# A decoder layer: the last group's output product by channel blocks over seven banks, tile 0 normed first, and the first scores by quarters

## The chip, the cores and the metric

The kernel runs on 1 core of one Trainium2 chip. The metric is the device time of one execution in microseconds. The engines are TensorE (PE, matmuls; PEld its weight loads), VectorE (DVE), ScalarE (ACT), GpSimd (POOL) and the queue of SyncE (SP), which issues most transfers.

## The reference

One post-norm decoder layer on 16 sequences of 56 tokens (896 rows of 512 values, all float32), with three parts, each followed by a layer norm of x + part:

```python
# 1. a state-space mixer: 128 heads of 64, 8 groups
h = x * rsqrt(mean(x*x) + 1e-5) * norm_w
gate, hBC, dt = split(h @ in_proj_w.T)            # 8192, 8192 + 2*1024, 128
hid, B, C = split(silu(causal_conv4(hBC) + conv_b))
dt = softplus(dt + dt_bias);  A = -exp(A_log)
y = ((C @ B.T) * exp(segsum(A * dt))) @ (hid * dt) + Dp * hid   # per head, causal
yg = y * silu(gate)
yg = yg * rsqrt(mean over each of the 8 groups of 1024 channels (yg*yg) + 1e-5) * gnorm_w
x = layernorm(x + (x + yg @ out_proj_w.T))
# 2. attention of the 56 tokens over a context of 1500 rows, context both key and value
x = layernorm(x + softmax(x @ ctx.T) @ ctx)
# 3. x @ W_base.T + b_base plus the two best of 8 low-rank experts (rank 16)
x = layernorm(x + base + lora)
```

## The kernel before, in words

**Mixer.** The 896 tokens are 7 tiles of 128 (TT = 7). The 8192 inner channels are 8 groups of 8 blocks of 128 (GROUPS, CT). For each group g and step st, PE projects one block of hid and one of gate (L1132), and for the block before it transposes hid (`transpose_hid`, L1143), DVE scales it (`scale_hid`) and weighs the decay matrix (`weigh`), and PE makes the block's y (`y_product`, L1156). DVE adds the skip term (`add_skip`, L794), then multiplies by the gate (`multiply_gate`, L807). To multiply in full precision with fast matmuls, y and the output weights are split in a high and a low part: ACT makes y_hi (L582) and wo_hi (L600), DVE wo_lo (L814), POOL y_lo (L414). ACT squares y (L593) and POOL adds the squares (L421).

**Output product.** It is y times w_out, three matmuls (high-high, high-low, low-high) for each token tile and channel block. For each group it goes in two halves of four blocks. `first_half` (step 5) goes tile by tile over two PSUM banks, `ob`, and ACT copies each tile to `part`. `second_half(g)` does the blocks 4 to 7 of group g - 1 in step 1 of group g: all four blocks of a tile, then the next tile, in the two banks in turn, so that a tile waits for DVE to have read the one two before it. Before it, PE sums the squares over the channels with a matrix of ones (`sum_squares`, L1192), from which DVE (`group_squares`) and POOL (`group_rms`, L426) make the group's scale rg. For each tile DVE adds the two halves (L875) and adds rg times them to `acc` (L878). The last group has its second half in a pseudo-group 8 of two steps (`group(GROUPS, 2)`), in which no projection runs.

**Norm 1 and attention.** In that pseudo-group, after each tile's sum, DVE makes the layer norm's statistics (`norm1_stats`, L899 to L904), POOL the scale and shift (L476, L478) and ACT the normed tile (`first_norm`, L673). The attention goes over 8 pairs of sequences. A pair's tokens are copied from `acc` to `x1p` by DMAs that POOL issues (`load_x1`, L460), padded to 64 rows a sequence. PE transposes them (`turn_queries`, L1203), and ACT spreads them over qT with 16 copies of 32 rows (`queries`, L687), quarter by quarter (c of 0 to 3). The context comes in units of 2 MB (three a pair, a ring of six: ring_a, ring_b) from SP (`load_unit`, L340). DVE transposes each unit in 32 by 32 blocks to keysT (`keys_part(u, r, half)`, two instructions, L886). PE makes the scores with 128 products of 32 rows by 64 columns, each over 384 keys and run as two instructions, in four row strips (`score`, L1285). DVE takes the maximum (`score_max`, L966), ACT the exponential (L703), PE transposes it (`turn_probs`, L1324) and multiplies by the context (`values`, L1336), DVE adds x1p (`norm2_sum`, L980). The feed-forward part of a pair runs under the scores and values of the next.

The order of the work is written out by hand for each engine; semaphores join the engines. In a pair, PE does score(u), turn_x2(u-1), turn_queries(u+1), feed_forward(u-1), turn_probs(u, 0 to 2), values(u, 0 to 2). DVE does the norms of pair u-1, keys_part(u+1, 0, 0), score_max(u), keys_part(u+1, 0, 1), the first probabilities' copy, the routing, four more key parts, and norm2_sum(u). POOL does rstd2(u-1), load_x1(u+1), rstd3 and the store of pair u-2. PSUM has eight banks: 0 to 3 take projections and later scores and transposed probabilities, 4 and 5 take y and later `turn` and `pv`, 6 and 7 are `ob` and later `ffn` and `misc`.

## Time and profile before

| | |
|---|---|
| median of 3 runs (lowest, highest) | 1488.67 us (1488.58, 1489.81) |
| the profiled execution, its time | 1492.33 us |
| the profiled execution, its span | 1490.6 us |
| mean granted TensorE clock | 0.981 |
| last projection's matmul starts | 1169.09 us |
| six context transfers (6 MB) are issued from | 1170.07 us |

The page gives for each engine its busy time, its share of the span and the number of instructions. A granted clock of 1.00 is 2.4 GHz, 0.50 is 1.2 GHz. Timelines give start (us from the span's start), duration, engine, line, operation, written and read tiles, and in brackets the idle time before with what ended it. Some matmul records can be missing.

**Single operations** in that trace (us):

| operation | duration |
|---|---|
| add_skip L794, two instructions | 1.27 |
| weigh L847; multiply_gate L807 | 1.08; 1.09 |
| scale_hid L825, two instructions | 1.29 |
| wo_lo L814: median, longest of 64 | 0.75, 2.58 |
| y_hi L582; sq L593 (ACT) | 0.95; 0.94 |
| y_lo L414; squares' sum L421 (POOL) | 2.08; 2.09 |
| transposes of hid L1143, eight | 1.07 |
| sum of squares at full clock L1192, eight | 0.59 |
| group_squares L860, L863, L865 | 0.39, 0.39, 0.17 |
| half sum L875; sum L878 | 0.69; 0.75 |
| statistics L899, L901, L903, L904 | 0.69, 0.18, 0.15, 0.15 |
| POOL's rstd L476; shift L478 | 0.56; 0.19 |
| first_norm L673 | 0.81 |
| transposes L1203, four | 0.66 |
| maximum L966; exponential L703 with its accumulator read | 1.76; 1.54 + 0.19 |
| x1p load's issue L460, three on POOL | 1.73 |

### The profile page before, as it was taken

The numbers are of one execution on the slowest core, as the hardware profiler recorded it, in microseconds if no ns is written. First come the engines' busy times: TensorE is split into PE (matmuls) and PEld (weight loads), VectorE is DVE, ScalarE is ACT, GpSimd is POOL, SyncE is SP. The second block draws the span as 40 slices with busy tenths as digits, with TensorE's granted clock in tenths as the row PEclk, the third lists the DMA queues.
The fourth block names the chain that finished last, engine by engine and source line by source line (L and its number), as shares of the span: only waits on it lengthen the run. The fifth ranks groups of instructions, "written<-read, shape, count | busy, mean of one in ns | idle before, by whom it ended". The sixth has DMA issues, their size and how long they took to land.

```text
span 1490.6 us, 29598 instructions
## 1 busy us (share of the span) xinstructions
PE 1424.6 (96%) x12540; PEld 1164.9 (78%) x12540; DVE 996.9 (67%) x1312; ACT 751.9 (50%) x1003; POOL 501.6 (34%) x368
## 2 busy tenths in 40 slices
PE   5899999999999999999999999999999779999895
PEld 4798989898889888888988898989898554445452
DVE  5774768476847675676577566747683776888764
ACT  5764636563746364636554564455455344533340
POOL 5252435242534243433343343425243320112001
PEclk9999999999999999999999999999999889999997
DMA  4431213121312131222122221222130455566600
GB/s 149 121 104 53 80 56 99 54 89 42 97 58 86 46 102 54 73 58 89 55 72 65 83 72 54 84 64 86 40 97 23 184 202 207 207 255 259 178 19 13
DMA packets 53345, 142.57 MB, mean 96 GB/s; under 512 B 9777, under 2 KB 9905, under 8 KB 46951
## 3 DMA queue, kind: packets, MB, share of 16 engines
q1 hardware_dynamic: 51518, 137.01, 27.9%
q0 software_dynamic: 1696, 3.67, 0.8%
q8 instruction: 99, 1.62, 0.5%
q14 instruction: 32, 0.26, 0.1%
HBM read 136.53 MB, written 2.29 MB: 93 GB/s over the span
## 4 chain that ended last, share of the span: by engine, by line
PE 85%; issue 7%; DVE 4%; DMA 2%; ACT 1%; POOL 1%; POOLq 0%; ACTq 0%; DVEq 0%
PE bank L1113 46%; PE bank L1181 21%; PE bank L1156 5%; PE bank L1143 4%; PE bank L1336 3%; PE bank L1285 2%; PE bank L1309 2%; DMA x1p<-acc 1%; DVE conv L780 1%; PE bank L1305 1%; PE bank L1168 1%; PE bank L1324 0%; DVE part L741 0%; DMA part<-in_x 0%; PE bank L1192 0%
## 5 line engine op out<-in xcount | busy, mean ns | idle before, releaser
L1113 PE MATMUL bank<-h_hi,w_hi 128*128 128x448 f32 x1152 | 338.1, 375 | 2.2 <-DVE conv L780 2.2
L414 POOL TENSOR_TENSOR y_lo<-yg,y_hi 128x896 fp32r<-128x896 f32 x64 | 136.2, 2127 | 581.5 <-ACT y_hi L582 541.4
L1113 PE MATMUL bank<-h_lo,w_hi 128*128 128x448 f32 x1152 | 328.0, 366 | 0.0
L1113 PE MATMUL bank<-h_hi,w_lo 128*128 128x448 f32 x1152 | 327.2, 365 | 0.0
L780 DVE SCALAR_TENSOR_TENSOR conv<-bank,conv_w,conv 128x880 f32<-128x880 f32 (+2 forms) x240 | 267.9, 1117 | 85.2 <-ACT conv L555 79.4
L1113 PEld LDWEIGHTS bank<-h_hi,w_lo 128*128 128x128 f32 x1152 | 216.8, 188 | 17.4
L1113 PEld LDWEIGHTS bank<-h_lo,w_hi 128*128 128x128 f32 x1152 | 216.9, 188 | 17.1
L398 POOL TENSOR_TENSOR w_lo<-w_raw,w_hi 128x512 fp32r<-128x512 f32 x144 | 188.3, 1308 | 119.0 <-ACT w_hi L521 117.5
L1113 PEld LDWEIGHTS bank<-h_hi,w_hi 128*128 128x128 f32 x1152 | 208.2, 188 | 20.0 <-DVE conv L780 2.6
L825 DVE TENSOR_TENSOR hd_dt<-bank,dt_j 128x512 f32<-128x512 f32 x128 | 82.3, 685 | 209.0 <-PE bank L1143 209.0
L1181 PE MATMUL bank<-wo_hi,y_hi 128*128 128x512 f32 x448 | 178.6, 399 | 7.9 <-POOL y_lo L414 3.8
L1181 PE MATMUL bank<-wo_lo,y_hi 128*128 128x512 f32 x448 | 176.5, 394 | 0.0
L1181 PE MATMUL bank<-wo_hi,y_lo 128*128 128x512 f32 x448 | 176.0, 393 | 0.0
L582 ACT ACTIVATE y_hi<-yg 128x896 fp32r<-128x896 f32 x64 | 60.9, 951 | 205.0 <-DVE yg L807 204.7
L562 ACT ACTIVATE hid<-conv 128x896 f32<-128x896 f32 x64 | 61.0, 953 | 150.4 <-DVE conv L780 150.2
L421 POOL TENSOR_TENSOR sqsum<-sq,sqsum 128x896 f32<-128x896 f32 x56 | 119.8, 2140 | 0.0
L1181 PEld LDWEIGHTS bank<-wo_hi,y_hi 128*128 128x128 f32 x448 | 85.1, 190 | 29.9 <-issue 6.2
L555 ACT ACTIVATE conv<-bank,conv_b,conv_w 128x896 f32<-128x896 f32 x80 | 87.0, 1088 | 31.7 <-PE bank L1113 31.6
L1285 PE MATMUL bank<-keysT,qT 32*64 32x384 f32 (+1 forms) x2048 | 88.0, 485 | 13.2 <-DVE keysT L886 9.6
L1181 PEld LDWEIGHTS bank<-wo_hi,y_lo 128*128 128x128 f32 x448 | 85.2, 190 | 18.3
L1181 PEld LDWEIGHTS bank<-wo_lo,y_hi 128*128 128x128 f32 x448 | 85.3, 190 | 17.1
L1285 PEld LDWEIGHTS bank<-keysT,qT 32*64 32x64 f32 x2048 | 52.0, 133 | 49.7 <-issue 33.0
(161 smaller groups left out, 1884.7 us busy)
## 6 DMA issues: line engine op xcount, KB each, us to landing
w_raw<-in_w_in SPq DMA_DIRECT2D x144, 256.0 KB, 2.9
decay<-cs_scratch SPq DMA_DIRECT2D x128, 196.0 KB
ring_a<-in_context SPq DMA_DIRECT2D x24, 1024.0 KB, 8.6
ring_b<-in_context SPq DMA_DIRECT2D x21, 1024.0 KB
wo_raw<-in_w_out SPq DMA_DIRECT2D x64, 256.0 KB, 2.7
ring_b<-in_context SPq DMA_DIRECT2D x3, 896.0 KB
acc<-in_x SPq DMA_DIRECT2D x1, 1792.0 KB, 9.2
out<-z POOLq DMA_DIRECT2D x16, 112.0 KB, 3.4
```

The source lines that it names most:

```text
L398: g_.tensor_tensor(w_lo[:, slot, :], w_raw[:, slot, :], w_hi[:, slot, :].bitcast(f32), ALU.subtract).then_inc(s["w_low"], 1)
L414: g_.tensor_tensor(y_lo[:, c % 4, :], yg[:, c % 2, :], y_hi[:, c % 4, :].bitcast(f32), ALU.subtract).then_inc(s["y_low"], 1)
L421: g_.tensor_tensor(out=sqsum[:], in0=sq[:], in1=sqsum[:], op=ALU.add).then_inc(s["sqsum_done"], 1)
L555: a(seqs(conv[:, m % 2, :]), bank_seqs(proj[idx % 2]), ACT.Identity, bias=conv_b[:, bass.ds(col, 1)], scale=conv_w[:, bass.ds(col, 1), TAP ...
L562: a(real(dst), seqs(conv[:, m % 2, :]), ACT.Silu).then_inc(s["silu_done"], 1)
L582: a(y_hi[:, c % 4, :], yg[:, c % 2, :], ACT.Copy).then_inc(s["y_high"], 1)
L780: v.scalar_tensor_tensor(out=dst[:, :, sh:LEN], in0=src[:, :, 0:LEN - sh], scalar=conv_w[:, bass.ds(col, 1), TAPS - 1 - sh], in1=dst[:, :, ...
L825: v.tensor_tensor(hd_dt[:, 4 * r:4 * r + 4, :].rearrange("p q (h d) -> p q h d", h=2), yt[:, r, :].rearrange("p (q h d) -> p q h d", q=4, ...
L1113: last = mm(place, w[:, k * P:(k + 1) * P], x[:, k, half * HALF:(half + 1) * HALF], start=(k == 0 and i == 0), stop=(k == KT - 1 and i == 2))
L1156: last = mm(yt[HD * h:HD * (h + 1), b, pair * PAD:pair * PAD + LEN], hd_dt[own_rows, pair, HD * h:HD * (h + 1)], mixw[own_rows, h, pair, : ...
L1181: last = mm(ob[:, b, :], y[:, c, tok], w[:, c, :], start=(c == 0 and i == 0), stop=(c == 3 and i == 2))
L1285: last = mm(scores[PAD * q:PAD * (q + 1), row, :].rearrange("p (j i) -> p j i", i=SQ)[:, :, 0:n], qT[lo:lo + SQ, b // 4, b % 4, PAD * q:PA ...
```

## The change

1. **Order of the output product.** Blocks 4 to 7 of the last group have seven PSUM banks, one for each token tile (`last_bank`). They go block by block: block 4 and part of block 5 are spread between the last projection, the transposes of hid and the two last y_products; then the rest of block 5, block 6 of six tiles, the sum of squares, block 7 of six tiles, and all of tile 6. The sum of squares reads three square tiles (sqsum, sq and a new sq_last), 24 instructions for 8, and POOL no longer adds the last two. DVE, no longer POOL, makes the last block's y_lo.
2. **Order on DVE, POOL and ACT.** Tile 0 alone gets its sum, statistics and norm first. Then DVE adds the halves of tiles 1 to 3, transposes unit 1, adds the halves of 4 to 6, transposes unit 2, and finishes tiles 1 and 2. The sums of tiles 3 to 6 and the statistics of tile 3 come at the end of pair 0, before norm2_sum(0); the statistics of tiles 4 to 6 at the end of pairs 1 to 3, before norm2_sum. POOL and ACT follow with `ln1_scale` and `first_norm`.
3. **First queries.** Pair 0 lies in tile 0. Its queries come from `acc` by four products with a new matrix `spread`, which transposes and pads, not from x1p.
4. **First scores.** The keys of units 0 and 1 are taken quarter by quarter of the queries (`q0_part`), then those of unit 2: 256 instructions of 256 columns and 256 of 128 columns for 256 of 384.
5. **Transfers.** Several SBUF tiles change places. Unit 0 is issued in the last step of the last group, before the last block of output weights; unit 1 after the last silu and `weigh`; unit 2 after the last add_skip. Units 3 to 5 are issued when the output product is done, and the weights of the feed-forward part after all sums.

The diff, cut to its core:

```diff
+        last_bank = (0, 1, 2, 3, 6, 7, 5)
...
+                    if g == LAST and st == CT - 1:
+                        sp.wait_ge(s["cb_done"], GROUPS)
+                        sp.wait_ge(s["d_done"], GROUPS * CT)
+                        sp.wait_ge(s["m_done"], GROUPS * CT - 2)
+                        load_unit(0)
                     load_wo(g, st)
...
+            over_groups(sp, group)
+            sp.wait_ge(s["silu_done"], GROUPS * 10)
+            sp.wait_ge(s["m_done"], GROUPS * CT)
             load_unit(1)
-            sp.wait_ge(s["cb_done"], GROUPS)
+            sp.wait_ge(s["yres_done"], GROUPS * CT)
             load_unit(2)
             sp.wait_ge(s["outb_done"], GROUPS * TT)
-            sp.wait_ge(s["sum_done"], GROUPS * TT)
             for unit in range(KR, RING):
                 load_unit(unit)
+            sp.wait_ge(s["sum_done"], GROUPS * TT)
+            sp.wait_ge(s["q_tr"], 1)
...
+            g_.memset(spread[:], 0.0).then_inc(s["pool_step"], 1)
+            pool.wait_ge(s["consts_set"], 1)
+            pool.wait_ge(s["pool_step"], 3)
+            for q in range(2):
+                last = g_.tensor_copy(spread[:, PAD * q:PAD * q + LEN], ident[:, LEN * q:LEN * (q + 1)])
+            last.then_inc(s["spread_set"], 1)
...
+            y_low(LAST, CT - 2)
+            group_rms(GROUPS)
...
+            ln1_scale(0)
...
+            load_x1(0)
+            ln1_scale(1)
+            ln1_scale(2)
+            load_x1(1)
...
+                if u + 3 < TT:
+                    ln1_scale(u + 3)
...
+            wo_high(LAST, CT - 2)
+            y_high(LAST, CT - 2)
+            squares(LAST, CT - 2)
+            wo_high(LAST, CT - 1)
+            y_high(LAST, CT - 1)
+            a(sq_last[:], yg[:, (CT - 1) % 2, :], ACT.Square).then_inc(s["sq_done"], 1)
...
+            first_norm(0)
+            queries(0, range(4))
+            first_norm(1)
+            first_norm(2)
...
+            def last_halves(t):
+                dve.wait_ge(s["outb_done"], LAST * TT + t + 1)
+                if t == 0:
+                    dve.wait_ge(s["outa_evac"], GROUPS * TT)
+                v.tensor_tensor(part[:, t, :], bank[:, last_bank[t], :], part[:, t, :],
+                                ALU.add).then_inc(s["psum_added"], 1)
+            def last_sum(t):
+                dve.wait_ge(s["psum_added"], LAST * TT + t + 1)
+                dve.wait_ge(s["rg_done"], GROUPS)
+                v.scalar_tensor_tensor(out=acc[:, t, :], in0=part[:, t, :], scalar=rg[:, t:t + 1],
+                                       in1=acc[:, t, :], op0=ALU.mult, op1=ALU.add).then_inc(s["sum_done"], 1)
...
+            add_skip(LAST, CT - 2)
+            weigh(LAST, CT - 1)
+            scale_hid(LAST, CT - 1)
+            multiply_gate(LAST, CT - 2)
+            wo_low(LAST, CT - 2)
+            keys_part(0, 0, 0)
+            add_skip(LAST, CT - 1)
+            multiply_gate(LAST, CT - 1)
+            wo_low(LAST, CT - 1)
+            dve.wait_ge(s["y_high"], GROUPS * CT)
+            v.tensor_tensor(y_lo[:, 3, :], yg[:, 1, :], y_hi[:, 3, :].bitcast(f32),
+                            ALU.subtract).then_inc(s["y_low_last"], 1)
+            keys_part(0, 0, 1)
+            group_squares(GROUPS)
+            last_halves(0)
+            last_sum(0)
+            norm1_stats(0)
+            for t in range(1, 4):
+                last_halves(t)
+            dve.wait_ge(s["psum_added"], LAST * TT + 4)
+            v.memset(bank[:, 3, 0:KJ * SQ].rearrange("p (j i) -> p j i", i=SQ)[:, :, KP - 3 * SQ:SQ],
+                     LOWEST).then_inc(s["lowest_set"], 1)
+            for half in range(2):
+                keys_part(0, 1, half)
+            for t in range(4, TT):
+                last_halves(t)
+            for half in range(2):
+                keys_part(0, 2, half)
+            for t in range(1, 3):
+                last_sum(t)
+                norm1_stats(t)
...
+                    for t in range(3, TT):
+                        last_sum(t)
+                if u + 3 < TT:
+                    norm1_stats(u + 3)
...
+            def sum_last_squares():
+                pe.wait_ge(s["yres_done"], GROUPS * CT)
+                pe.wait_ge(s["sqsum_done"], 7 * LAST + CT - 3)
+                for n, squares in enumerate((sqsum, sq, sq_last)):
+                    if n:
+                        pe.wait_ge(s["sq_done"], LAST * CT + CT - 2 + n)
+                    for i in range(P // SUB):
+                        last = mm(bank[SUB * i:SUB * (i + 1), 4, 0:TT * SUB].rearrange("p (t a) -> p t a", a=SUB),
+                                  ones[:], squares[:].rearrange("p (t i a) -> p i t a", t=TT, a=SUB)[:, i],
+                                  start=(n == 0), stop=(n == 2))
+                last.then_inc(s["ss_done"], 1)
+            def last_part(t, c):
+                tok = slice(t * P, (t + 1) * P)
+                for i, (y, w) in enumerate(((y_hi, wo_hi), (y_hi, wo_lo), (y_lo, wo_hi))):
+                    last = mm(bank[:, last_bank[t], :], y[:, c % 4, tok], w[:, c % 4, :], start=(c == 4 and i == 0),
+                              stop=(c == 7 and i == 2))
+                return last
+            def last_ready(c):
+                wait(pe, s["wo_low"], CT, LAST, c + 1)
+                if c == CT - 1:
+                    pe.wait_ge(s["y_low_last"], 1)
+                else:
+                    wait(pe, s["y_low"], CT, LAST, c + 1)
...
+            def turn_first_queries():
+                pe.wait_ge(s["x1_set"], 1)
+                pe.wait_ge(s["ss_picked"], GROUPS)
+                pe.wait_ge(s["spread_set"], 1)
+                for k in range(KT):
+                    last = mm(turn[:, k * P:(k + 1) * P], acc[:, 0, k * P:(k + 1) * P], spread[:],
+                              start=True, stop=True)
+                last.then_inc(s["q_tr"], 1)
...
+                        last_ready(4)
+                        last_part(4, 4)
+                        last_part(5, 4)
...
+            pe.wait_ge(s["conv_tap"], GROUPS * 30)
+            last_part(0, 4)
+            last_part(1, 4)
+            transpose_hid(LAST, CT - 1)
+            pe.wait_ge(s["gate_done"], GROUPS * CT)
+            last_part(2, 4)
+            last_part(3, 4)
+            last_ready(5)
+            last_part(4, 5)
+            y_product(LAST, CT - 1)
+            for t in (5, 0, 1, 2, 3):
+                last_part(t, 5)
+            last_ready(6)
+            for t in range(6):
+                last_part(t, 6)
+            sum_last_squares()
+            last_ready(7)
+            for t in range(6):
+                last_part(t, 7).then_inc(s["outb_done"], 1)
+            for c in range(4, 7):
+                last_part(6, c)
+            last_part(6, 7).then_inc(s["outb_done"], 1)
+            turn_first_queries()
+            def score_block(b, j0, j1):
+                for row in range(4):
+                    lo, n = SQ * row, min(SQ, KP - SQ * row)
+                    for q in range(2):
+                        last = mm(scores[PAD * q:PAD * (q + 1), row, :].rearrange("p (j i) -> p j i", i=SQ)[:, j0:j1, 0:n],
+                                  qT[lo:lo + SQ, b // 4, b % 4, PAD * q:PAD * (q + 1)],
+                                  keysT[lo:lo + SQ, q, b, j0:j1, 0:n], start=(b == 0), stop=(b == NB - 1))
+                return last
+            def score_first():
+                pe.wait_ge(s["lowest_set"], 1)
+                pe.wait_ge(s["psum_added"], LAST * TT + 4)
+                for c in range(4):
+                    if c < 3:
+                        pe.wait_ge(s["q0_part"], c + 1)
+                    else:
+                        pe.wait_ge(s["q_set"], 1)
+                    if c == 0:
+                        pe.wait_ge(s["kT_set"], 8)
+                    for k in range(KT):
+                        score_block(4 * k + c, 0, 2 * KB)
+                pe.wait_ge(s["kT_set"], 12)
+                for b in range(NB):
+                    last = score_block(b, 2 * KB, KJ)
+                    if b % 8 == 7:
+                        last.then_inc(s["s_mm"], 1)
```

## Rows read from the trace of the kernel before

**Rows 1.** The page: busy time by engine, and the queue of instructions.

```profile
PE 1424.6 (96%) x12540; PEld 1164.9 (78%) x12540; DVE 996.9 (67%) x1312; ACT 751.9 (50%) x1003; POOL 501.6 (34%) x368
...
q8 instruction: 99, 1.62, 0.5%
```

**Rows 2.** Windows: length, busy us (instructions) by engine, PE clock, DMA share, GB/s.

```profile
1169.60:1178.60 9.00, 3.36 (x137) 2.89 (x136) 6.23 (x8) 4.28 (x6) 2.26 (x2) 0.99 0.88 349
1178.60:1195.70 17.10, 11.91 (x33) 7.85 (x34) 13.28 (x19) 1.79 (x2) 8.87 (x6) 0.51 0.49 201
1195.70:1210.00 14.30, 14.25 (x65) 11.44 (x63) 12.70 (x31) 6.00 (x9) 7.04 (x16) 1.00 0.11 34
1210.00:1219.60 9.60, 0.01 (x2) 0.04 (x2) 9.46 (x13) 9.43 (x16) 1.00 (x4) 0.63 0.74 285
1219.60:1235.30 15.70, 12.72 (x260) 7.58 (x260) 7.92 (x7) 2.41 (x4) 0.00 (x0) 0.90 0.85 346
```

**Rows 3.** Timeline of PE, 1164 to 1300: start, us, operation, [idle before].

```profile
1169.58 1.15 PE L1156 MATMUL bank<-mixw,hd_dt 64*64 64x56 f32 x64
...
1179.12 0.76 PE L1181 MATMUL bank<-wo_hi,y_hi 128*128 128x512 f32 x1 [3.63 <-DVE wo_lo L814]
...
1187.05 0.79 PE L1181 MATMUL bank<-wo_hi,y_hi 128*128 128x512 f32 x1 [3.75 <-POOL y_lo L414]
...
1189.10 0.98 PE L1192 MATMUL bank<-sqsum,ones 128*32 128x224 f32 x8 [0.41 <-POOL sqsum L421]
...
1209.56 0.39 PE L1181 MATMUL bank<-wo_hi,y_lo 128*128 128x512 f32 x1
1219.59 12.15 PE L1285 MATMUL bank<-keysT,qT 32*64 32x384 f32 x256 [9.64 <-DVE keysT L886]
...
1235.32 1.84 PE L1324 MATMUL bank<-ident,probs 128*128 128x128 f32 x12 [2.99 <-ACT probs L703]
...
1248.86 10.56 PE L1285 MATMUL bank<-keysT,qT 32*64 32x384 f32 x256
...
1260.46 0.66 PE L1203 MATMUL bank<-ident,x1p 128*128 128x128 f32 x4 [0.45 <-DMA x1p<-acc]
...
1290.42 0.66 PE L1203 MATMUL bank<-ident,x1p 128*128 128x128 f32 x4 [0.57 <-DMA x1p<-acc]
```

**Rows 4.** Timeline of DVE, 1148 to 1300.

```profile
1176.91 4.56 DVE L814 SCALAR_TENSOR_TENSOR wo_lo<-wo_raw,gnorm,wo_hi 128x512 fp32r<-128x512 f32 x2 [1.63 <-ACT wo_hi L600]
...
1198.61 0.69 DVE L875 TENSOR_TENSOR part<-bank,part 128x512 f32<-128x512 f32 x1
...
1201.33 0.69 DVE L875 TENSOR_TENSOR part<-bank,part 128x512 f32<-128x512 f32 x1
...
1212.58 9.12 DVE L886 STREAM_TRANSPOSE keysT<-ring_a 128x1024 f32<-128x1024 f32 x8
...
1231.84 1.76 DVE L966 TENSOR_REDUCE smalls<-bank 128x1 f32<-128x1536 f32 x1 [2.76 <-PE bank L1285]
...
1249.04 0.75 DVE L980 SCALAR_TENSOR_TENSOR x<-bank,smalls,x1p 128x512 f32<-128x512 f32 x1 [3.26 <-issue]
```

**Rows 5.** Timelines of ACT (first row) and POOL, 1148 to 1300.

```profile
1207.21 9.58 ACT L687 ACTIVATE qT<-bank 32x512 f32<-32x512 f32 x16 [1.44 <-PE bank L1203]
...
1191.24 1.48 POOL L426 TENSOR_TENSOR rg<-ms,epsc 128x7 f32<-128x7 f32 x1 [2.19 <-DVE ms L865]
...
1251.53 1.73 POOL L460 DMA_DIRECT2D x1p<-acc  x3
```

**Rows 6.** Tile x1p: landings of loads issued 1196 to 1250, then 1240 to 1280.

```profile
DMA to landing us min/median/max: 2.1/2.2/3.0
...
DMA to landing us min/median/max: 5.9/6.6/7.7
```

**Rows 7.** Waits from 1160 on: us in total, times, longest.

```profile
PE bank L1203 <- DMA x1p<-acc: 2.6, 4, 0.8
```

**Rows 8.** Timeline of the queue of SP, 1140 to 1380.

```profile
1211.54 2.86 SPq L340 DMA_DIRECT2D ring_b<-in_context  x6
```

More of the change, by code:

```diff
@@ L941, in group @@
                             add_output(g, t)
-                            if not live:
-                                norm1_stats(t)
-                    if live and st == 0:
+                    if st == 0:
                         mask_cb(g)
             over_groups(dve, group)
-            group(GROUPS, 2)
-            for r in range(1, KR):
-                for half in range(2):
-                    keys_part(0, r, half)
+            add_skip(LAST, CT - 2)
[29 more added lines that the diff above has]
+                norm1_stats(t)
             steps = [1]
@@ L1281, in score @@
                         pe.wait_ge(s["kT_set"], 12 * u + 12)
-                    for row in range(4):
-                        lo, n = SQ * row, min(SQ, KP - SQ * row)
-                        for q in range(2):
-                            last = mm(scores[PAD * q:PAD * (q + 1), row, :].rearrange("p (j i) -> p j i", i=SQ)[:, :, 0:n],
-                                      qT[lo:lo + SQ, b // 4, b % 4, PAD * q:PAD * (q + 1)],
-                                      keysT[lo:lo + SQ, q, b, :, 0:n], start=(b == 0), stop=(b == NB - 1))
+                    last = score_block(b, 0, KJ)
                     if b % 8 == 7:
```

119 lines of the change are left out of this document (48 added, 71 removed).

## The prediction

> **What bounds the kernel now.** I read the page first, then the stretch around the change in windows, then the timelines of TensorE (PE), VectorE (DVE), ScalarE (ACT) and GpSimd (POOL) there, and last the landings of x1p. The profiled span is 1490.6 us in an execution of 1492.33 us, 3.66 us above the median of 1488.67 of the runs. I make the sum on the span and take its difference off the median. PE is busy for 96% of the span [rows 1], so almost any gain must come from a place where PE is idle or slow. The change touches one such place, between the last input projection (about 1169.6) and the first transposes of the probabilities (1235.3). There PE is busy 42.25 of 65.7 us (3.36 + 11.91 + 14.25 + 0.01 + 12.72), so it idles 23.45 us, and the granted clock is 0.51 from 1178.6 to 1195.7 and 0.63 from 1210.0 to 1219.6 [rows 2]. PE waits 3.63 us for wo_lo, 3.75 us for POOL's y_lo, and 9.64 us at the end for the transposed keys: DVE normed all seven tiles before it transposed eight more key pieces from 1212.58 on [rows 3, 4]. After that PE is the bound in every pair of sequences, with one short wait in some of them: for x1p [rows 3, 7].
>
> **The new order up to the first queries.** All times are on the span's scale. Durations of single operations that stand in no row are those of the table of single operations above. One "piece" (a token tile by a channel block) is three matmuls. From 1195.7 to 1210.0 PE was busy for 14.25 us with 65 matmuls, four of them small transposes [rows 2]: (14.25 - 0.4) / 61 = 0.227 us a matmul, 0.68 us a piece. PE starts two pieces (1.36 us), y_product of block 6 (1.1 us), two pieces: 1173.5. Block 6's add_skip on DVE starts 1.36 us later than before, ends at 1173.45, and the transposes follow at once (0.9 us): 1174.4. Three more pieces: 1176.4. Y_product of block 7 (1.1 us): 1177.5; five pieces: 1180.95; six pieces of block 6: 1185.05. The sum of squares is now 24 matmuls in place of 8, which took 0.98 us at half the clock [rows 3]; I take 1.1 us for all at the full clock, bounds 0.5 and 2.9. Six pieces of block 7 and four of tile 6: 6.8 us, end at 1193.0. Before, it was 1209.95 [rows 3]. Block 7 must be ready at 1186.1. DVE: scale_hid to 1175.8, gate 1176.9, wo_lo 1177.6, key piece 2.4 us to 1180.0, add_skip, gate, wo_lo to 1182.9 (ACT copies y_hi meanwhile, to 1183.2), and then the subtraction y_lo, which DVE takes over from POOL: 1.1 us, the price of the equally large gate product; bounds 1.1 and the 2.1 us of POOL. It ends at 1184.3, 1.8 us before PE needs it. The second of the two last wo_lo took 2.58 instead of 0.75 us in the old run (the pair lasts 4.56 us with the wait between them, [rows 4]); if that returns, it takes up the whole 1.8 us.
>
> DVE then has a key piece until 1186.7, the group's squares (1.1 us), POOL's rg takes 1.49 us [rows 5] to 1189.4, then sum and statistics of tile 0 (2.0 us, being the 2.72 us of a tile from row to row in [rows 4] less the 0.72 us half sum): 1191.4. POOL's scale (0.85 us) and ACT's norm (0.8 us) end at 1193.15. So the four products with the spread matrix start at 1193.2, with PE just done, and replace a trip of x1p through the DMA; 0.7 us (as the four transposes), bounds 0.6 and 1.2. ACT's 16 query copies take 9.58 us [rows 5]: a quarter is there at 1196.3, all at 1203.5.
>
> **The first scores.** DVE adds three half sums (2.2 us), sets the padding and transposes unit 1 (four pieces, 9.12/8 = 1.14 us each [rows 4], 4.6 us): 1198.2. The unit left the queue when m_done was full (1174.4), so it has landed long before; unit 2 leaves at 1181.2. So scores start at 1198.2 and not at 1219.59. PE idles 4.3 us before them. Three half sums and unit 2 take DVE to 1205.0. In the old run 256 matmuls of 384 columns took 10.56 us, 41 ns each [rows 3], which is their columns at the full clock with four row groups side by side. The first part has 256 matmuls of 256 columns: 6.9 us, but its last quarter waits for 1203.5, so it ends at 1205.2. The second part has 256 matmuls of 128 columns: 13.7 ns by columns, or 17 ns by the 64 small matmuls in about 1.1 us of y_product [rows 3]. I take 17: 4.35 us, bounds 3.4 and 10.5 (the old price per instruction). Scores end at 1209.6, or up to 3.4 us later if the first part falls to half the clock after the idle 4.3 us.
>
> The Trainium skill, "TensorE: Matmul & The Clock Gate", section "Wait — 56ns, not 53.3ns?", says that start-to-start never drops below about 25 ns however few the columns. By that rule the second part would take 6.4 us. The trace disagrees for matmuls that lie side by side: 17 ns.
>
> DVE: sum and statistics of tiles 1 and 2 to 1209.0, a key piece pair of unit 3 to 1211.4, and only then the maximum (1.76 us): 1213.2. So DVE, not PE, sets this, which hides 1.8 us of late scores. The exponential ends 1.7 us later, and turn_probs starts at 1215.0; I take 1215.5 for a part of the slow clock. Before, 1235.32 [rows 3]: **19.8 us gained**.
>
> Turn_queries(1) stands ahead of turn_probs in PE's order. Its x1p load follows the scale of tile 2 in POOL's order and leaves at 1210.0 to 1211.6. Unloaded it lands 2.1 to 3.0 us later, among context loads 5.9 to 7.7 [rows 6]. Units 3 to 5 (6.3 MB) now leave at 1193.0 instead of 1211.54 [rows 8] and need 15.5 us at 346/0.85 = 407 GB/s [rows 2]: gone by 1210. So it lands by 1214.6, under the wait for the exponential. Without that cover it costs 3 to 4 us.
>
> **What is given back.** The four last sums (3.1 us) and the norm statistics of tile 3 (1.2 us) now stand in front of norm2_sum(0) on DVE, behind eight key pieces that end at 1226.0: norm2_sum starts at 1230.3, and score(1) at 1215.5 + 13.5 = 1229.0 (13.54 us as before, [rows 3]). Before, it started 0.2 us after score(1) [rows 3, 4]. So x1p for pair 2 leaves about 1.2 us later against PE, and PE already waited 0.45 us for it [rows 3]: 1.2 us lost. The statistics of tiles 4, 5 and 6 do the same in pairs 1 to 3. Pair 2 had waited 0.57 us for x1p (1.2 lost); the next two did not wait, since the four waits of all pairs are 2.6 us together [rows 7], so I count 0.4 and 0.7. Sum: **3.5 us given back**, bounds 0 and 6. The FFN weights now wait for all sums (1229.1 instead of 1214) and units 6 to 8 wait behind them: weights there at 1236, needed at 1240; unit 6 at 1240, so the maximum of pair 1 is done at 1244.0 and its exponential at 1245.8, beside 5.5 us of PE work until about 1247. That costs nothing with 1.2 us to spare. ACT's later norms fall into its idle time.
>
> Sum: 19.8 - 3.5 = 16.3 us. Span 1474.3 us; time 1488.67 - 16.3 = **1472.4 us**.
>
> **Rivals.** (a) The pair loop gives nothing back: its x1p loads leave later and land as before. For it: unloaded, a landing takes 2.1 to 3.0 us and not 5.9 to 7.7 [rows 6], and a load that leaves later meets less of the context traffic. Time 1488.67 - 19.8 = 1468.9. (b) x1p for pair 1 meets the context loads or comes late, 4 us, and x1p of the four pairs after it waits fully, 6 us in all: 19.8 - 10 = 9.8, time 1478.9. Against it: the queue should be empty at 1210. (c) The 25 ns rule holds for the second part: scores end at 1211.7, the maximum starts 0.3 us later, time 1472.7; the rule is named above, and y_product's rows speak against it. (d) Slower: PE's instruction stream is too slow. The first scores are now 512 matmuls and as many weight loads beside full DMA queues, and instructions come over a queue too (q8, 1.62 MB, [rows 1]). Planned are 22 ns a matmul; 16.3 us over 512 are 32 ns, so from 54 ns each the kernel is no faster. At 70 ns it would be 8 us slower than before, 1497. Against it: 41 ns a matmul was kept in old scores under equal loads [rows 2, 3].
>
> **How the numbers follow.** Chances: forecast 0.65, (a) 0.12, (b) 0.15, (c) 0.04, (d) 0.04. The earliest that bounds allow is a gain of 21 us (1467.7). The late side is (b) with a wo_lo of 2.6 us not covered and 1.6 us of slow clock: a gain of 7 (1481.7). The range 1467 to 1482 leaves out (d) and tails. A measurement of this kernel tells 0.2%, 3 us, from no change: faster 0.96, same 0.01, slower 0.03.
>
> **What would show it.** The last matmul of the output product near 1193; scores starting near 1198; DVE's maximum starting near 1211.5 right behind a key piece; turn_probs near 1215.5; scores of pair 1 near 1229, and of pair 2 near 1260 with a wait of some 1.6 us for x1p. The prediction fails if PE waits for y_lo at 1186, if a context unit lands after DVE asks for it, if turn_queries(1) starts after 1215, or if the pairs from 4 on take another time than before.

## The result, and the profile after

The changed kernel takes 1479.07 us (median of 4 runs, 1477.87 to 1480.21), the kernel before 1488.62 us (4 runs, 1486.96 to 1489.81): 9.6 us less, a ratio of 0.9937 with a 95% interval of 0.9925 to 0.995. The forecast was 1472.4 us, in a range of 1467 to 1482. So the direction and the range held, but the gain is 9.6 us where 16.3 were forecast. The profiled execution took 1479.15 us, its span is 1477.4 us. The span of the profiled execution before is 1490.6 us, so the two traces lie 13.2 us apart; but that execution's time was 3.7 us above its median.

The timeline of PE after the change, in the columns of [rows 3]:

```profile
1185.45 0.58 PE L1265 MATMUL bank<-sqsum,ones 128*32 128x224 f32 x8
...
1193.44 0.39 PE L1274 MATMUL bank<-wo_hi,y_lo 128*128 128x512 f32 x1
1193.67 1.05 PE L1298 MATMUL bank<-spread,acc 128*128 128x128 f32 x8
1198.10 7.98 PE L1392 MATMUL bank<-keysT,qT 32*64 32x256 f32 x221 [3.37 <-DVE keysT L934]
1207.06 2.60 PE L1392 MATMUL bank<-keysT,qT 32*64 32x232 f32 x128 [0.98 <-issue]
1213.27 4.29 PE L1392 MATMUL bank<-keysT,qT 32*64 32x116 f32 x163 [3.61 <-issue]
1217.49 0.66 PE L1289 MATMUL bank<-ident,x1p 128*128 128x128 f32 x4
1221.07 1.53 PE L1463 MATMUL bank<-ident,probs 128*128 128x128 f32 x12 [2.93 <-ACT probs L730]
...
1233.45 10.56 PE L1392 MATMUL bank<-keysT,qT 32*64 32x384 f32 x256
...
1248.49 1.11 PE L1289 MATMUL bank<-ident,x1p 128*128 128x128 f32 x4 [3.90 <-DMA x1p<-acc]
```

Up to 1198.10 nearly every step came out as forecast. The output product ends at 1193.8 (forecast 1193.0, before 1209.95 [rows 3]), the 24 squares' matmuls need 1.3 us (forecast 1.1), and the scores start at 1198.10 instead of 1219.59: 21.5 us sooner. Then the scores of pair 0 take 19.4 us and not 11.4. They have gaps of 0.98 and 3.61 us whose bracket says "issue": PE waited for nothing that the profile knows, neither a semaphore nor a transfer of data. And between the scores of pair 1 and those of pair 2 lies a wait of 3.90 us for x1p.

DVE, the columns as in [rows 4], and the queue of SP, as in [rows 8]:

```profile
1182.96 1.09 DVE L989 TENSOR_TENSOR y_lo<-yg,y_hi 128x896 fp32r<-128x896 f32 x1 [0.36 <-ACT y_hi L605]
...
1214.80 2.37 DVE L934 STREAM_TRANSPOSE keysT<-ring_b 128x1024 f32<-128x1024 f32 x2 [6.87 <-PE bank L1392]
1217.60 1.76 DVE L1022 TENSOR_REDUCE smalls<-bank 128x1 f32<-128x1536 f32 x1 [0.42 <-PE bank L1392]
...
1231.42 2.70 DVE L923 SCALAR_TENSOR_TENSOR acc<-part,rg,acc 128x512 f32<-128x512 f32 x4
...
1235.29 0.75 DVE L1036 SCALAR_TENSOR_TENSOR x<-bank,smalls,x1p 128x512 f32<-128x512 f32 x1
...
1250.63 2.37 DVE L934 STREAM_TRANSPOSE keysT<-ring_a 128x1024 f32<-128x1024 f32 x2 [12.24 <-DMA ring_a<-in_context]
```

```profile
1193.87 3.46 SPq L350 DMA_DIRECT2D ring_b<-in_context  x6
1234.15 0.33 SPq L369 DMA_DIRECT2D wbT<-in_w_base  x1
...
1236.87 3.30 SPq L350 DMA_DIRECT2D ring_a<-in_context  x6
```

The maximum of pair 0 starts at 1217.60 (forecast 1211.4), since it had to wait for the scores. The four sums stand at 1231.42, and SP, which waits for them, issues the weights at 1234.15 and six transfers of units 6 to 8 from 1236.87 on, almost at once. Before, units 6 to 8 left one by one behind the values. DVE gets unit 6 at 1250.63; the forecast was 1240. The same transfers in the queue of SP before (first row) and in e5 below, the kernel in which this was mended (second row):

```profile
1242.11 7.67 SPq L340 DMA_DIRECT2D ring_a<-in_context  x6
```

```profile
1224.24 8.10 SPq L350 DMA_DIRECT2D ring_a<-in_context  x6
```

They left 6.8 and 7.2 us before the scores of pair 1 began (1248.86 and 1231.41). In the changed kernel they left 3.4 us after that.

The later pairs on PE:

```profile
1270.50 7.98 PE L1392 MATMUL bank<-keysT,qT 32*64 32x384 f32 x191
1279.16 2.83 PE L1392 MATMUL bank<-keysT,qT 32*64 32x348 f32 x65 [0.68 <-issue]
...
1282.85 0.66 PE L1289 MATMUL bank<-ident,x1p 128*128 128x128 f32 x4 [0.28 <-DMA x1p<-acc]
...
1313.01 0.66 PE L1289 MATMUL bank<-ident,x1p 128*128 128x128 f32 x4 [0.61 <-DMA x1p<-acc]
...
1343.33 0.66 PE L1289 MATMUL bank<-ident,x1p 128*128 128x128 f32 x4 [0.64 <-DMA x1p<-acc]
```

A gap of "issue" (0.68 us) stands in the scores of pair 2 as well, whose matmuls are the old ones.

Where the 13.2 us of the two traces lie, by the start of each pair's scores:

| from | to | before | after | gain |
|---|---|---|---|---|
| start | scores of pair 0 | 1219.59 | 1198.10 | 21.5 |
| scores 0 | scores 1 | 29.27 | 35.35 | -6.1 |
| scores 1 | scores 2 | 29.84 | 37.05 | -7.2 |
| scores 2 | scores 5 (three pairs) | 91.08 | 91.07 | 0.0 |
| scores 5 | scores 6 | 30.22 | 29.84 | 0.4 |
| scores 6 | scores 7 | 36.61 | 32.89 | 3.7 |
| scores 7 | end | 53.99 | 53.10 | 0.9 |

### The profile page after: what moved, and what is told of

Read it like the earlier page. It is cut to its first block, busy times and chain, and to the rows that moved or that the text cites. A ratio compares the mean times of both kernels' runs of the same rounds, so it can differ in the third digit from the quotient of the medians.

```text
span 1477.4 us, 30164 instructions
## 1 busy us (share of the span) xinstructions
PE 1420.3 (96%) x12816; PEld 1169.2 (79%) x12816; DVE 993.2 (67%) x1313; ACT 752.2 (51%) x1003; POOL 496.0 (34%) x368
## 3 DMA queue, kind: packets, MB, share of 16 engines
q8 instruction: 101, 1.65, 0.5%
## 4 chain that ended last, share of the span: by engine, by line
PE 83%; DVE 7%; issue 4%; DMA 3%; ACT 1%; POOL 1%; SPq 0%; DVEq 0%; POOLq 0%; ACTq 0%
PE bank L1174 47%; PE bank L1242 20%; PE bank L1217 5%; PE bank L1204 4%; DVE keysT L934 3%; DMA x1p<-acc 2%; PE bank L1477 2%; PE bank L1392 2%; PE bank L1448 1%; DMA ring_a<-in_context 1%; PE bank L1274 1%; DVE conv L809 1%; PE bank L1229 1%; PE bank L1444 0%; DVE part L770 0%
## 5 line engine op out<-in xcount | busy, mean ns | idle before, releaser
L1242 PE MATMUL bank<-wo_hi,y_hi 128*128 128x512 f32 x420 | 165.2, 393 | 0.0
L1242 PE MATMUL bank<-wo_lo,y_hi 128*128 128x512 f32 x420 | 163.7, 390 | 0.0
L1242 PE MATMUL bank<-wo_hi,y_lo 128*128 128x512 f32 x420 | 163.4, 389 | 0.0
L439 POOL TENSOR_TENSOR sqsum<-sq,sqsum 128x896 f32<-128x896 f32 x54 | 115.2, 2133 | 0.0
L1392 PE MATMUL bank<-keysT,qT 32*64 32x384 f32 (+5 forms) x2304 | 90.2, 457 | 9.8 <-issue 6.3
L1242 PEld LDWEIGHTS bank<-wo_hi,y_hi 128*128 128x128 f32 x420 | 78.8, 188 | 19.1 <-issue 2.5
L1242 PEld LDWEIGHTS bank<-wo_hi,y_lo 128*128 128x128 f32 x420 | 78.9, 188 | 16.6
L1392 PEld LDWEIGHTS bank<-keysT,qT 32*64 32x64 f32 x2304 | 59.1, 137 | 41.6 <-issue 27.5
L1242 PEld LDWEIGHTS bank<-wo_lo,y_hi 128*128 128x128 f32 x420 | 78.9, 188 | 15.8
```

What stands on the lines that cost most here:

```text
L439: g_.tensor_tensor(out=sqsum[:], in0=sq[:], in1=sqsum[:], op=ALU.add).then_inc(s["sqsum_done"], 1)
L1242: last = mm(ob[:, b, :], y[:, c, tok], w[:, c, :], start=(c == 0 and i == 0), stop=(c == 3 and i == 2))
L1392: last = mm(scores[PAD * q:PAD * (q + 1), row, :].rearrange("p (j i) -> p j i", i=SQ)[:, j0:j1, 0:n], qT[lo:lo + SQ, b // 4, b % 4, PAD * ...
```

## The experiments

Two places had to be explained: the gaps in the first scores (-6.1) and pair 1 (-7.2). Theory 1 is that PE's instructions arrive too slowly there. Theory 2 is that weights and three units in one burst make unit 6 and x1p late. Where a range stands behind a time, the time is the median of four runs; the others are single executions. Several chips were used: the kernel before had a median of 1488.62 us (seven runs) beside e0 to e3, of 1487.56 us (seven runs) beside e4 to e7, and took 1491.97 us (one run) beside e8 and e9.

**e0: the kernel before once more.**

> The kernel before, unchanged, profiled once more. In its first trace the stretch from the scores of pair 6 (1400.00) to those of pair 7 (1436.61) took 36.6 us, against 29.8 to 31.0 us for the pairs before it, and 32.9 us in the changed kernel. If this is chance of one execution, the new trace shows some 32 to 34 us there and a time near 1488.6; if it belongs to the kernel, it shows 36.6 us again and the change gained 3.7 us there.

Its span is 1485.9 us and its time 1487.67. The scores of pair 6 again had a gap of "issue":

```profile
1397.13 9.91 PE L1285 MATMUL bank<-keysT,qT 32*64 32x384 f32 x235
1409.81 2.58 PE L1285 MATMUL bank<-keysT,qT 32*64 32x384 f32 x21 [2.77 <-issue]
```

From there to the scores of pair 7 it took 35.7 us (36.6 in the first trace). So most of the 3.7 us in that stretch belongs to the kernel. In the ten kernels with the change the stretch took 32.2 to 35.6 us, in seven of them 32.2 to 32.9. The gap is there in all ten, but shorter (0.80 to 1.64 us) and at another matmul, behind the 213th of 256 (in e8 the 217th) and not the 235th. The first traces of before and of the changed kernel:

```profile
1412.78 1.56 PE L1285 MATMUL bank<-keysT,qT 32*64 32x384 f32 x21 [2.87 <-issue]
```

```profile
1401.68 2.16 PE L1392 MATMUL bank<-keysT,qT 32*64 32x384 f32 x43 [1.03 <-issue]
```

That is 1.8 of the 3.7 us. No step of the prediction said so, and why the gap shrank, and the rest, stay open.

**e1: pair 0's scores in one pass.**

```diff
-                for c in range(4):
-                    if c < 3:
-                        pe.wait_ge(s["q0_part"], c + 1)
...
-                    for k in range(KT):
-                        score_block(4 * k + c, 0, 2 * KB)
+                pe.wait_ge(s["q_set"], 1)
                 pe.wait_ge(s["kT_set"], 12)
                 for b in range(NB):
-                    last = score_block(b, 2 * KB, KJ)
+                    last = score_block(b, 0, KJ)
```

> The changed kernel, but pair 0's scores go in one pass of 256 matmuls of 384 columns once all queries and all keys are there. In the changed kernel the two passes took 19.4 us from 1198.1, with gaps of 1.0 and 3.6 us that no semaphore explains. Theory 1 (PE's instructions arrive too slowly beside the context loads; the two passes use them up at twice the rate): one pass starts near 1204.4, runs 10.6 to 12 us with at most 1 us of gaps, ends at 1215 to 1216.5, and the time falls by 1 to 2.5 us against the changed kernel. Rival (the loads slow any scores there, by their access to SBUF): one pass has the same 4.6 us of gaps, ends near 1220, and the time rises by 2 to 3 us.

1477.03 us (1475.27 to 1478.47), ratio 0.9928 (0.9909 to 0.9948), 2.0 us under the changed kernel; the two intervals overlap, so the sign of this difference is not certain. PE:

```profile
1203.13 11.93 PE L1392 MATMUL bank<-keysT,qT 32*64 32x384 f32 x256 [9.91 <-ACT qT L712]
...
1218.65 1.96 PE L1455 MATMUL bank<-ident,probs 128*128 128x128 f32 x12 [3.01 <-ACT probs L730]
```

There is no gap in the pass, beside the same context loads. It starts 5 us later than the two passes and ends 2.5 us sooner. Of these 2.5 us 1.5 are not its own: this trace already lies that much earlier at the spread product (1192.16 for 1193.67), where the kernels are still the same. So the loads do not slow every score; the two passes have a trouble of their own. But one pass only avoids it, and wins next to nothing by that: from the spread product to the scores of pair 1 it takes 40.0 us, the two passes 39.8 in the changed kernel and 41.9 in e7 below, which has two passes as well.

**e2: no context load beside the two passes.** SP waits for the end of pair 0's scores before unit 3.

```diff
             sp.wait_ge(s["outb_done"], GROUPS * TT)
+            sp.wait_ge(s["s_mm"], 2)
             for unit in range(KR, RING):
```

> The changed kernel, but units 3 to 5 of the context are issued only when pair 0's scores are done, so that no context load runs beside the two passes. Theory 1: no gaps over 0.5 us in the two passes, second pass at about 17 ns a matmul, scores end at 1209.6 to 1211. Rival (the two passes are bound by something of their own, such as a fixed cost of a short matmul or of a switch between parts): gaps and the end near 1217.5 stay. The total is expected about 3 us worse than the changed kernel or equal, since the key pieces of pair 1 wait for unit 3.

1485.3 us. PE and one window of it (DMA share 0.06):

```profile
1196.48 11.49 PE L1393 MATMUL bank<-keysT,qT 32*64 32x256 f32 x349 [3.36 <-DVE keysT L935]
1208.30 2.07 PE L1393 MATMUL bank<-keysT,qT 32*64 32x116 f32 x128 [0.33 <-issue]
1212.05 0.82 PE L1393 MATMUL bank<-keysT,qT 32*64 32x116 f32 x35 [1.67 <-issue]
```

```profile
1196.40:1212.90 16.50, 14.42 (x513) 12.42 (x514) 9.71 (x17) 9.14 (x14) 3.55 (x7) 0.81 0.06 17
1196.40:1202.40 6.00, 5.92 (x114) 5.07 (x122) 6.00 (x7) 5.86 (x11) 0.00 (x0) 0.50 0.02 3
1202.40:1208.10 5.70, 5.58 (x243) 4.81 (x228) 3.71 (x11) 2.02 (x4) 2.78 (x6) 0.99 0.01 3
```

The scores took 16.4 us: 3.0 less than beside the loads, but 5 more than forecast. Of these 5 us the clock makes 3: it was 0.50 for the first 6 us, behind the 3.36 us in which PE was idle. The gaps make the other 2. Theory 1 expected no gap over 0.5 us, and that failed: gaps of 0.33 and 1.67 us are left. The rows show why. Between the gaps lies one chunk of 128 matmuls, and it ran in 2.07 us, 16 ns a matmul: the price of a short matmul was right. What is slow is the supply from chunk to chunk. The total was 6.2 us worse than the changed kernel, not 3 at most: DVE waited for unit 3 until 1221.45, and PE 13.74 us for the exponential behind it. The changed kernel shows the same chunk of 128 before its second gap, and the queue of instructions has one packet at just that time (the first fence is the DMA view from 1210.6 to 1211.8, the second from 1214 to 1215.5; after the queue and its kind stand its packets, the MB and the share of 16 engines, context loads being q1):

```profile
q1 hardware_dynamic: 59, 0.48, 97.9%
q8 instruction: 1, 0.02, 5.4%
```

```profile
q8 instruction: 1, 0.02, 3.6%
```

PE resumed at 1213.27, behind the first of these. From the start of these scores to 1220 the queue of instructions has four packets, near 1204.5, 1210.5, 1214 and 1218: 6 us apart beside the loads, 3.5 to 4 us without. And the gaps keep to a count, not to a time. Of 512 matmuls they stand behind the 221st and 349th (changed kernel), behind these and the 477th (e3, e7), behind the 349th and 477th (e2), each time at steps of 128. 128 matmuls and their 128 weight loads are 256 instructions. The Trainium skill, "Runtime: NRT & Kernel Launch", section "Instruction fetch mechanics", says that an engine's instructions are refilled in blocks of 16 KiB, 256 instructions; the packets of 0.02 MB and the chunks of 128 agree. It also says that this is mostly hidden; here it is not.

**e9: three passes, 256 matmuls more.**

```diff
                     for k in range(KT):
-                        score_block(4 * k + c, 0, 2 * KB)
+                        score_block(4 * k + c, 0, KB)
+                for c in range(4):
+                    for k in range(KT):
+                        score_block(4 * k + c, KB, 2 * KB)
```

> The changed kernel with pair 0's scores in three passes, one for each context unit: 768 matmuls of 128 columns, the same columns in all, 256 matmuls more than two passes. Theory 1 (128 matmuls and their 128 weight loads are one block of instructions, and a block takes about 4 us without context loads and about 6 us beside them): two blocks more, so the scores take 8 to 12 us more than the 19.4 of two passes and have one or two gaps more, each a few us, with chunks of 128 matmuls between gaps. Rival (the gaps come from something that two passes have twice at most, such as a change between parts or a wait that the profile does not show): no more than 4 us more.

1485.05 us. The scores took 26.3 us, 6.9 more than in two passes, with the same columns in all. That is 1.1 us under what theory 1 expected, and clear of the rival's 4. All of it lies behind the first gap, which is again behind the 221st matmul. The last four chunks on PE:

```profile
1207.17 3.72 PE L1392 MATMUL bank<-keysT,qT 32*64 32x116 f32 x128 [0.85 <-issue]
1213.11 6.60 PE L1392 MATMUL bank<-keysT,qT 32*64 32x116 f32 x256 [2.22 <-issue]
1220.60 2.07 PE L1392 MATMUL bank<-keysT,qT 32*64 32x116 f32 x128 [0.89 <-issue]
1224.35 0.81 PE L1392 MATMUL bank<-keysT,qT 32*64 32x116 f32 x35 [1.68 <-issue]
```

After each gap PE runs 128 or 256 matmuls and stops again (behind the 221st, 349th, 605th and 733rd of 768). Soon after 1213 the context loads are over, and three blocks take 11.24 us (1213.11 to 1224.35): 3.7 us each. So two added blocks cost some 7 us.

**e3: the sums of tiles 3 to 6 before the pair loop.**

```diff
             for t in range(1, 3):
                 last_sum(t)
                 norm1_stats(t)
+            for t in range(3, TT):
+                last_sum(t)
...
-                if u == 0:
-                    for t in range(3, TT):
-                        last_sum(t)
```

> The changed kernel, but the sums of tiles 3 to 6 stand on DVE before the pair loop (in its idle 6.9 us while pair 0's scores run) and not before norm2_sum(0). So the weights of the feed-forward part are issued at about 1212 instead of 1234, and units 6 to 8 follow the values of pair 0. Theory 2 (pair 1's 37.05 us against 29.84 before come from weights and three units issued in one burst behind those sums, which makes unit 6 and x1p land late): the stretch from the scores of pair 1 to those of pair 2 takes 30 to 31 us, and the time falls by 6 to 7 us, to about 1472.5. Rival (the norm statistics before norm2_sum set it): the stretch stays over 34 us and the time falls by less than 3 us.

1476.99 us (1475.07 to 1481.13), ratio 0.9928 (0.9907 to 0.995). Pair 1 took 30.75 us instead of 37.05 and had no wait for x1p, as theory 2 expects. But the time fell by 2.1 us and not by 6 to 7. The profiled execution, the slowest of the four, shows why:

```profile
1207.72 2.60 PE L1391 MATMUL bank<-keysT,qT 32*64 32x232 f32 x128 [1.68 <-issue]
1213.94 3.02 PE L1391 MATMUL bank<-keysT,qT 32*64 32x116 f32 x128 [3.61 <-issue]
1220.42 1.42 PE L1391 MATMUL bank<-keysT,qT 32*64 32x116 f32 x35 [3.47 <-issue]
```

The weights now leave at 1210.92 and lengthen the loads beside the two passes, so that a third block of instructions comes late as well (3.47 us), and the scores take 23.4 us. That execution was 4.1 us above the median, so the loss in the others is probably smaller. And e7 below has a third gap too, of 1.67 us, without the weights beside it.

**e5: one pass and early sums together.**

> The changed kernel with both edits at once: pair 0's scores in one pass, and the sums of tiles 3 to 6 before the pair loop. Theory 1 (instructions come in blocks, and two passes outrun them) and theory 2 (the burst behind the late sums) have different places, so their gains add: scores of pair 0 from 1203 to 1216 without a gap over 0.6 us, pair 1 to pair 2 in 30 to 31 us, time 1470 to 1472.5. Rival for the first place (the weights, now issued at 1211, hold up the instructions in one pass too): a gap of 2 to 3.5 us before the scores end, time near 1474.5.

1470.66 us (1469.85 to 1472.47), ratio 0.989 (0.9871 to 0.9908): 8.4 us better than the changed kernel (7.0 by the ratios to the kernel before on each chip) and the best of all. Scores of pair 0 from 1202.99 to 1215.43 without a gap, pair 1 in 30.97 us. Alone they brought 2.0 and 2.1 us. The reason is in the traces, from the spread product to the scores of pair 1, then pair 1:

| kernel | to the scores of pair 1 | pair 1 |
|---|---|---|
| changed kernel | 39.8 | 37.05 |
| e7 (two passes) | 41.9 | 35.6 |
| e1 (one pass) | 40.0 | 35.0 |
| e3 (early sums) | 44.8 | 30.75 |
| e5 (both) | 39.4 | 30.97 |

The early sums win the 6 us of pair 1, and with two passes they lose up to 5 us of it before, in the supply of instructions; one pass wins little by itself and keeps that loss away. Of the 9.3 us between the traces of e5 and the changed kernel another 1.65 us lie before the spread product (1192.02 for 1193.67), where nothing was edited. The traces of the kernels with the change scatter there from 1191.95 to 1194.41, and why is open.

**e4: the burst kept.** As e5, with one wait more on SP before the weights:

```diff
             sp.wait_ge(s["q_tr"], 1)
+            sp.wait_ge(s["v_mm"], KR)
```

> One pass and early sums, but SP holds the weights of the feed-forward part back until the values of pair 0 are done, so that weights and units 6 to 8 leave in one burst near 1230 as in the changed kernel, while DVE's norm2_sum(0) is as early as with early sums. Theory 2 (the burst itself does the harm): pair 1 to pair 2 takes 34 to 37 us again, with DVE waiting some 10 us for unit 6. Rival (the late norm2_sum and so the late issue of x1p do it): 31 us or less.

1478.19 us; pair 1 takes 36.66 us although norm2_sum(0) is at 1232.18, 0.2 us after the scores of pair 1 start, as in the kernel before. The waits of 1225 to 1262, in the columns of [rows 7]:

```profile
DVE keysT L935 <- DMA ring_a<-in_context: 12.8, 1, 12.8
...
PE bank L1289 <- DMA x1p<-acc: 2.0, 1, 2.0
```

So what SP's queue does makes the pair long, and not DVE's order. DVE waits for unit 6, its maximum is late, and PE waits 3.66 us for the exponential. Two things go together in the burst and no run separates them: units 6 to 8 leave late (1235.25, 3.3 us after the scores of pair 1 began), and they leave all at once behind the weights (unit 6 lands 11.1 to 13.3 us after its issue in the changed kernel, 4.9 to 7.0 us in e5). The wait for x1p is another matter: it is 3.90 us in the changed kernel, 2.00 here and 1.58 in e5, so DVE's late sums made about half of it. It ends before the wait for the exponential, so it does not set the length of the pair.

**e6: norm statistics in DVE's idle time.** As e5, and in DVE's pair loop:

```diff
+                if u + 3 < TT:
+                    norm1_stats(u + 3)
                 if u < PAIRS:
                     score_max(u)
...
-                if u + 3 < TT:
-                    norm1_stats(u + 3)
                 if u < PAIRS:
                     norm2_sum(u)
```

> As the kernel with one pass and early sums, but the norm statistics of tiles 3 to 6 stand before the maximum of their pair, where DVE waits for the scores, and not before norm2_sum. The prediction's step (1.2 us later x1p costs PE up to 1.2 us in pairs 1 to 3): waits for x1p in pairs 1 to 4 fall by 1 to 3 us together and the time with them. Rival (x1p lands with the end of the context loads whenever it was issued within a us or so): no change over 0.7 us in the stretches of those pairs.

1472.01 us (1470.63 to 1472.68), ratio 0.9893 (0.9878 to 0.9909), not told apart from e5. Pairs 1 to 4 took 31.09, 30.37, 30.08 and 29.83 us, against 30.97, 29.85, 30.37 and 29.77 in e5. PE's waits for x1p fell from 3.8 to 2.5 us over all pairs, but small gaps of instructions took their place in two pairs (0.61 and 0.41). So nothing was gained there.

**e7: y_lo on POOL again.**

```diff
             y_low(LAST, CT - 2)
+            y_low(LAST, CT - 1)
...
-            v.tensor_tensor(y_lo[:, 3, :], yg[:, 1, :], y_hi[:, 3, :].bitcast(f32),
-                            ALU.subtract).then_inc(s["y_low_last"], 1)
...
```

> The changed kernel, but POOL makes the last block's y_lo again (about 2.1 us) instead of DVE (1.09 us). In the changed kernel y_lo was ready at 1184.0 and PE wanted it at 1186.7, so the prediction's cover is 2.7 us and the cost of the slower engine 1.0 us: the last matmul of the output product and the start of the scores move by less than 0.3 us, or the scores start up to 1 us sooner as DVE's next key piece is free earlier. Rival (it is on the critical path): both move by 1 us or more later.

1477.49 us. Its whole trace lies 1.42 us earlier from before the change's place on (POOL's y_lo of block 6 starts at 1176.29 instead of 1177.71). By that shift the first spread matmul (1192.26 for 1193.67) and the scores' start (1196.67 for 1198.10) stand where they stood. The slower engine is fully covered. Its first scores took 20.4 us with gaps of 1.61, 3.61 and 1.67, so the gaps are no accident of one trace.

**e8: pair 0's queries by the DMA.** As e5, with transposes of x1p for the spread product:

```diff
-                pe.wait_ge(s["x1_set"], 1)
+                pe.wait_ge(x1_loaded[0], x1_landed(0))
...
-                    last = mm(turn[:, k * P:(k + 1) * P], acc[:, 0, k * P:(k + 1) * P], spread[:],
-                              start=True, stop=True)
+                    last = tr(turn[:, k * P:(k + 1) * P], x1p[:, 0, k * P:(k + 1) * P], ident[:])
```

> The kernel with one pass and early sums, but pair 0's queries come from x1p over the DMA and the four transposes, as before the change, and not from the spread product. There the scores start at 1203 with the last query copy. x1p for pair 0 is issued near 1192.5 and lands 2.1 to 3 us later or, beside units 3 to 5 issued at the same time, up to 5 us. If the direct product is worth its place, queries and scores come 2 to 5 us later and the time is 2 to 4.5 us worse; rival (hidden anyway by the keys of unit 2, ready near 1202.6): less than 1 us.

1480.51 us, 9.9 us over e5, where 2 to 4.5 were expected. The two were timed on different chips: by the ratios to the kernel before on the same chip (1480.51 to 1491.97, one run each, and 0.989) the difference is about 5 us. The trace is the better witness. PE, and the landings of x1p:

```profile
1200.37 1.11 PE L1296 MATMUL bank<-ident,x1p 128*128 128x128 f32 x4 [7.93 <-DMA x1p<-acc]
1211.39 11.98 PE L1389 MATMUL bank<-keysT,qT 32*64 32x384 f32 x256 [9.91 <-ACT qT L712]
```

```profile
DMA to landing us min/median/max: 6.3/6.7/7.1
```

The load runs beside units 3 to 5, and scores start 8.4 us later (1211.39 for 1202.99). So the direct product pays, by 8.4 us at the start of the scores. x1p needs 6.3 to 7.1 us here, where its loads at that place needed 2.1 to 3.0 us in the kernel before [rows 6], because the context now leaves at the same time. How the other parts of the change rank beside it was not measured.

## Why the prediction was right in direction and too high in size

**Up to the first scores: right.** The chain held to 0.8 us: last product 1193.8 (1193.0), y_lo ready 1184.0 (1184.3) and wanted at 1186.7 (1186.1), scores 1198.10 (1198.2). PE idled 3.4 us before the scores. e7 shows the cover of y_lo, e8 that the spread product pays.

**"Scores end at 1209.6": wrong, a mis-sized term.** Planned were 6.9 us and 4.35 us at 17 ns a matmul, 11.4 in all. Measured: 19.4 us, 38 ns a matmul. The 8.0 us more are two things. The gaps are 4.6 us. The rest is the clock, 0.60 and 0.50 in two stretches of the changed kernel:

```profile
1198.10:1202.30 4.20, 4.20 (x98) 4.09 (x106) 4.20 (x6) 4.09 (x8) 0.00 (x0) 0.60 1.02 365
...
1213.20:1215.70 2.50, 2.43 (x95) 2.43 (x99) 0.90 (x1) 0.00 (x0) 0.00 (x0) 0.50 0.06 21
```

The first 221 matmuls took 7.98 us where 27 ns each make 6.0: 2.0 us, behind the 3.37 us in which PE was idle. This the prediction allowed for (up to 3.4 us) and did not put in its sum. The last 163 took 4.29 us, against 2.9 at the full clock in e7: 1.4 us, behind the gap of 3.61 us. In e7 a third gap of 1.67 us stood in its place, so the slow clock there cost next to nothing of its own. Rival (d) named the mechanism of the gaps, PE's instruction stream, and was given 0.04 with a break-even at 54 ns. It came true in part: e1 avoids it, e9 makes it larger, and e2 shows that 2.0 us of the 4.6 stay without loads. What the argument against it missed: the old scores need 128 times 41 ns = 5.3 us for a block, the new ones 3.4 and 2.2 us. A block took 3.7 us without loads in e9, so the new rate was not sustainable. The old one nearly is: e1's pass beside the loads has no gap, and other pairs have some, of 0.2 to 2.9 us. How e1 kept pace although two gaps beside loads lay 6.2 us apart was not tested; its pass is only two blocks long and followed 9.9 us of waiting. The 17 ns were right for a matmul (16 ns in e2's chunk) and wrong for the whole run of 256, which needed its instructions as well. DVE's order could hide 1.8 us of it; turn_probs came at 1221.07 instead of 1215.5, 5.6 us late. Rival (c), 25 ns a matmul however short, does not hold for these side by side: 16 ns.

**"That costs nothing with 1.2 us to spare": wrong.** This was said of the weights and of units 6 to 8 behind the late sums. Unit 6 landed at 1250.6 instead of 1240, and pair 1 took 37.05 us instead of 31.0: 6 us lost. e3, e4 and e5 show that the burst is the cause. Of the 10.6 us by which unit 6 was late, 5.0 came with the late scores (the sums end at 1234.1 and not at 1229.1); the other 5.6 are the transfers'. The arithmetic took 407 GB/s and transfers strictly one after another. The windows of the changed kernel, in the columns of [rows 2]:

```profile
1234.00:1250.60 16.60, 12.71 (x265) 8.40 (x247) 3.52 (x11) 1.41 (x2) 2.99 (x6) 0.88 0.90 305
1236.80:1250.60 13.80, 9.90 (x196) 6.44 (x181) 0.89 (x3) 0.74 (x2) 2.26 (x4) 0.86 0.97 335
```

At 305 GB/s over 16.6 us, 5.1 MB had come when unit 6 was there, and only 3.9 MB (the weights and unit 6) stood ahead of its end; x1p makes 0.2 MB more. So the rate was lower, also once all transfers were out (335 GB/s with the engines busy at 0.97), and some 0.9 MB of units 7 and 8 came before unit 6 was complete. x1p for pair 2 left at 1237.8 and needed 7.7 to 9.5 us instead of 5.9 to 7.7 [rows 6] (6.2 to 8.8 in e5), and PE, idle for 3.9 us, ran at half its clock until about 1253.5.

**The pair loop's give-back: too high.** Pairs 2 to 4 lost 0.0 and not 2.3 us against the first trace before, and 1.4 us against that of e0 (89.71 us). So rival (a) was nearly right for them. PE waited 0.61 and 0.64 us for x1p in pairs 3 and 4, where it had not waited before, and e6 shows that less waiting for x1p does not shorten these pairs. x1p for pair 1 was in time, against rival (b): at 1217.49 PE did not wait. The median lies 0.2 us from the 1478.9 us of rival (b), and that is chance: its 10 us of waits for x1p did not come, the waits are 7.5 us in all against 2.6 before [rows 7].

**The tail.** 5.0 us came that no step named, 3.7 of them in the stretch from pair 6 to pair 7. Sum of the traces: 16.3 - 5.6 + 1.1 (pair 0 took 12.4 us from turn_probs to the next scores, not 13.5) - 6.0 + 2.3 + 5.0 = 13.1, against 13.2. By medians the gain is 9.6, because the profiled execution before was 3.7 us above its median.

## What to carry to other kernels

Splitting a matmul in two to start it sooner doubles its instructions; when each one's work falls to some 30 ns (here 3.7 us over the 128 matmuls of a block), count blocks of 256 instructions against the supply before you count columns. And where such a run starts behind a wait, put the slow clock into the sum and not only into its bounds. A late small step can hold a queue: ask of every wait on the transfer queue what leaves behind it all at once, and what small transfer must share that moment. Two such faults can hide each other's repair, so repair both before you judge one.

## What the runs showed of the hardware

- PE's instructions come in blocks of 256: gaps stand 128 or 256 matmuls apart at the same counts in five kernels, and the kernel before has 99 packets of 0.016 MB on that queue [rows 1] for 25080 matmuls and weight loads, 98 blocks. Without other transfers a block of short matmuls took 3.7 us (e9); beside context loads two gaps lay 6.2 us apart with one block between them (1207.06 to 1213.27); that the loads are what makes the difference rests on e2, where the same gaps shrank from 4.6 to 2.0 us. Short matmuls of 116 to 128 columns in 32 by 64 parts run at 16 ns in between.
- A small copy inside SBUF by POOL's queue lands 2.1 to 3.0 us after its issue when nothing else runs [rows 6], 6.3 to 7.1 us beside context loads (e8), and 7.7 to 9.5 us beside a burst of weights and units (6.2 to 8.8 us beside units that leave one by one, e5).
- Transfers issued close together on one queue are not finished strictly one after another: 5.1 MB had moved where 4.1 MB were due, x1p included.
- PE's clock was 0.50 for 6.0 us at the start of scores behind 3.36 us of idle time (e2), and 0.50 behind a gap of 3.61 us in the changed kernel; behind the same gap of 3.61 us in e7 it stayed at 1.00.
